# State-space stage of three of four token pairs moved beside the attention steps of a perceiver block

## The reference

```python
# 1. cross attention, for each of 8 batches: context (1024, 256), latents x (64, 256)
ln = _layernorm(latents); kv_input = concat([_layernorm(x), ln])
logits = einsum('bhld,bhsd->bhls', q * scale, k * scale)        # 16 heads of 64
out = softmax(logits) @ v ; return out @ Wo
# 2. state space model over the 64 tokens of a batch, 512 channels, 16 states
xc, z = split(layernorm(x) @ W_in);  xc = silu(conv4(xc));  dbc = xc @ x_proj_w
dt = softplus(dbc[..., :1] * dt_w + dt_b);  A = -exp(A_log)
h = exp(dt * A) * h + dt * B_t * x_t ;  y_t = einsum('bdn,bn->bd', h, C_t)
return ((y + xc * D) * silu(z)) @ W_out + residual
# 3. eight experts (256 -> 1024 -> 256, gelu) on listed tokens, scattered back with weights
```

## Time and profile before

| | us |
|---|---|
| median of 3 runs (lowest, highest) | 875.82 (875.15, 876.38) |
| the profiled execution, its own time | 878.02 |
| its span, first to last instruction | 876.3 |
| attention, 40.5 to 603.7 | 563.2 |
| state space, 603.7 to 789.0 | 185.3 |
| experts and end, 789.0 to 876.3 | 87.3 |

### The profile page before, as it was taken

One profiled execution on the slowest core, in us unless ns is written; L12 is line 12 of the kernel. 1 busy time (PEld: TensorE's weight loads), 2 busy tenths in 40 slices (PEclk: granted clock), 3 DMA queues, 4 the chain that ended last, 5 costly groups with the idle time before them and its releaser, 6 DMA issues.

```text
span 876.3 us, 13897 instructions
## 1 busy us (share of the span) xinstructions
PE 797.1 (91%) x5395; PEld 685.5 (78%) x5395; DVE 501.2 (57%) x1087; ACT 393.7 (45%) x947; POOL 263.2 (30%) x207
## 2 busy tenths in 40 slices
PE   4989999999999999999999999996837788889996
PEld 2679999999999999999999999995313233358895
DVE  5266465565466556456556554444687899970112
ACT  2445454544454554454554354441644444414341
POOL 2818017016105403501801700001045776620000
PEclk8999999999999999999999999998958999999998
DMA  9100100100010010010030010000200000081720
GB/s 312 59 1 1 55 1 1 54 2 2 1 55 2 1 55 1 1 56 1 2 127 1 4 8 2 1 1 3 96 1 0 1 0 0 1 287 31 262 93 27
DMA packets 23781, 35.28 MB, mean 40 GB/s; under 512 B 6744, under 2 KB 19616, under 8 KB 22688
## 3 DMA queue, kind: packets, MB, share of 16 engines
q1 hardware_dynamic: 23712, 34.34, 11.9%
HBM read 32.77 MB, written 0.52 MB: 38 GB/s over the span
## 4 chain that ended last, share of the span: by engine, by line
PE 76%; DVE 11%; issue 7%; POOL 2%; ACT 2%; DMA 1%; SPq 0%; DVEq 0%; POOLq 0%
PE psum L1182 21%; PE psum L1216 19%; PE psum L1199 6%; PE psum L1155 3%; PE psum L1508 3%; PE psum L1498 3%; PE psum L1238 3%; DVE read L805 2%; PE psum L1138 2%; PE psum L1310 2%; PE psum L1377 2%; PE psum L1162 2%; POOL drive L558 2%; PE psum L1248 2%; PE psum L1229 2%
## 5 line engine op out<-in xcount | busy, mean ns | idle before, releaser
L929 ACT ACTIVATE pt_hi<-psum 128x512 fp32r<-128x512 f32 (+1 forms) x192 | 87.3, 489 | 225.7 <-PE psum L1199 170.4
L1216 PE MATMUL psum<-kvn_hi,pt_hi 128*128 128x256 f32 x512 | 149.6, 292 | 0.0
L1216 PE MATMUL psum<-kvn_hi,pt_lo 128*128 128x256 f32 x512 | 144.1, 281 | 0.0
L1216 PE MATMUL psum<-kvn_lo,pt_hi 128*128 128x256 f32 x512 | 143.9, 281 | 0.0
L651 DVE TENSOR_REDUCE rowmax<-psum 128x1 f32<-128x728 f32 x64 | 58.6, 915 | 110.9 <-PE psum L1182 110.9
L558 POOL TENSOR_TENSOR drive<-dtx,b_all 128x512 f32<-128x512 f32 x64 | 82.9, 1301 | 49.0 <-DVE state L796 23.4
L1216 PEld LDWEIGHTS psum<-kvn_lo,pt_hi 128*128 128x128 f32 x512 | 97.2, 190 | 0.1
L1216 PEld LDWEIGHTS psum<-kvn_hi,pt_hi 128*128 128x128 f32 x512 | 97.1, 190 | 0.1
L1216 PEld LDWEIGHTS psum<-kvn_hi,pt_lo 128*128 128x128 f32 x512 | 97.0, 189 | 0.0
L1182 PE MATMUL psum<-kvt_hi,qk_hi 128*128 128x364 f32 (+1 forms) x384 | 90.8, 345 | 4.5 <-ACT prob L969 2.7
L1182 PE MATMUL psum<-kvt_hi,qk_lo 128*128 128x364 f32 (+1 forms) x384 | 85.5, 331 | 0.0
(11 more groups left out here) (205 smaller groups left out, 1494.7 us busy)
## 6 DMA issues: line engine op xcount, KB each, us to landing
w<-in_L_ffn_W_dram SPq DMA_DIRECT2D x16, 1024.0 KB, 7.5
ctx_nat<-in_ctx_dram SPq DMA_DIRECT2D x8, 1024.0 KB, 5.3
wk_nat<-in_L_xattn_Wkv_dram SPq DMA_DIRECT2D x1, 1024.0 KB, 6.1
wq_sb<-in_L_xattn_Wq_dram SPq DMA_DIRECT2D x1, 1024.0 KB, 12.3
wv<-in_L_xattn_Wkv_dram SPq DMA_DIRECT2D x1, 1024.0 KB, 14.4
wo<-in_L_xattn_Wo_dram SPq DMA_DIRECT2D x1, 1024.0 KB, 16.4
lat_cur<-x_lat SPq DMA_DIRECT2D x16, 64.0 KB, 4.9
q_t<-in_L_attn_W_in_dram SPq DMA_DIRECT2D x1, 1024.0 KB, 7.2
```

The source lines that it names most:

```text
L929: act.activation(pt_hi[u][:, t0:t1, :], where[:, 0:(t1 - t0) * P].rearrange("p (t m) -> p t m", m=P), ACT.Copy)\
L1216: pe.matmul(PV, w[u][:, j, :], x_[slot][:, j, :], start=(j == 0 and w is pt_hi and x_ is kvn_hi), stop=False)
```

## The change

The state-space work of pairs 0, 1 and 2 moves into the head steps of later batches; only pair 3 stays behind the attention.

- A unit is now one state of one pair: 4 channel tiles x 128 tokens, again 512 elements a partition. `unit_step` puts one unit in each of the head steps 26 to 57 (pairs 0 and 1), and two in each of the steps 58 to 65 (pair 2). Pair 3 has 16 units after the attention, with a loop like the one before.
- A unit beside the attention is: SP loads its row of B and of C from device memory, repeated over the partitions (`load_rows`, 128 KB); POOL makes the drive (`open_unit`); ACT makes the decay in SBUF with four exponentials (`decays`); DVE scans, with both inputs in SBUF (`scan_unit`); POOL multiplies with C and adds to the sum (`close_unit`, two operations).
- The work around the units of a pair stands at set steps after its base (19, 35, 51): norm and transposes (+1), `in_proj` (+2), convolution (+2, +3), the gate of the convolution (+4), `x_proj` (+5), dt (+5, +6), skip (+7), gate z (+12, +13; +8, +9 for pair 2), gating of the result and product with W_out (+23, +24). Silu is made of an exponential, a plus one, a DVE reciprocal of 128x512 (`invert`) and a product on POOL: two reciprocals a pair.
- Queries (`q_keep`), latents (`latt_keep`, `x_keep`) are stored to device memory and loaded by SP for each batch; this removes POOL's `queries` and ACT's `own_rows` after batch 0. qk has one buffer in place of two, and two of a batch's eight `misc` turns move into that batch's own steps 0 and 1.
- POOL's context work is cut up: norm at hp 2, a quarter of weight and bias at each of hp 3 to 6, high part at 6, low part at 7, latents at hp 0 of the next batch.

```diff
-    UNITS = DT * NS
...
+    TURNS = (0, 2, 4, 5, 6, 7, 1, 3)
+    EARLY, OWN_LATE, NEXT_LATE = {6: 5, 7: 7}, {0: 1, 1: 3}, {3: 0, 4: 2, 5: 4, 6: 6}
...
+    WORKS = 3
+    ROWS = 3
+    INLINE = TT - 1
...
+        def unit_step(u):
+
+            t, n = divmod(u, NS)
+            if t < INLINE - 1:
+                return 2 * HP * t + 26 + n
+            return 2 * HP * t + 26 + n // 2
...
+            def load_rows(u):
+
+                t, n = divmod(u, NS)
+                if u >= ROWS:
+                    sp.wait_ge(v_acc, u - ROWS + 1)
+                pair = dbc_keep[t % 2, 1:, :].rearrange("(a w n) p -> a w n p", a=1, n=NS)[:, :, n, :]
+                sp.dma_start(bc[u % ROWS][:], pair.to_broadcast((P, 2, P))).then_inc(ld_bc[u % ROWS], 16)
...
+            def open_unit(u):
+
+                t, n = divmod(u, NS)
+                pool.wait_ge(ld_bc[u % ROWS], 16 * (u // ROWS + 1))
+                if n == 0:
+                    pool.wait_ge(v_dtx, t + 1)
+                if u >= WORKS:
+                    pool.wait_ge(v_acc, u - WORKS + 1)
+                pool.tensor_tensor(work[u % WORKS][:], dtx[:], bc[u % ROWS][:, 0:1, :].to_broadcast((P, DT, P)),
+                                   ALU.mult).then_inc(v_drv, 1)
+
+            def close_unit(u):
+
+                t, n = divmod(u, NS)
+                pool.wait_ge(v_scan, u + 1)
+                link(pool.tensor_tensor(work[u % WORKS][:], work[u % WORKS][:],
+                                        bc[u % ROWS][:, 1:2, :].to_broadcast((P, DT, P)), ALU.mult))
+                if n == 0:
+                    pool.wait_ge(v_y0, t + 1)
+                else:
+                    pool.wait_ge(v_acc, u)
+                pool.tensor_tensor(y_sum[:], y_sum[:], work[u % WORKS][:], ALU.add).then_inc(v_acc, 1)
...
+                for u in units_at.get(g - 1, ()):
+                    close_unit(u)
+                for u in units_at.get(g, ()):
+                    open_unit(u)
...
+            def invert(t, made, done):
+
+                dve.wait_ge(made, t + 1)
+                dve.reciprocal(gate[:], gate[:]).then_inc(done, 1)
...
+            def scan_unit(u):
+
+                dve.wait_ge(v_dec, u + 1)
+                dve.wait_ge(v_drv, u + 1)
+                flat = "p d m -> p (d m)"
+                dve.tensor_tensor_scan(work[u % WORKS][:].rearrange(flat), dec[u % 2][:].rearrange(flat),
+                                       work[u % WORKS][:].rearrange(flat), 0.0, ALU.mult, ALU.add).then_inc(v_scan, 1)
...
+                for u in units_at.get(g, ())[:1]:
+                    scan_unit(u)
...
+                for d in range(DT):
+                    last = act.activation(seqs(dec[u % 2][:])[:, d, :, 1:], seqs(dts[:])[:, d, :, 1:], ACT.Exp,
+                                          scale=a_neg[:, d, n:n + 1])
+                last.then_inc(v_dec, 1)
...
+            pool.wait_ge(s_woe, TT)
+            token_norm(INLINE)
+            for u in units_at[HP * B + 1]:
+                close_unit(u)
+            times_gate(INLINE - 1)
+            link(pool.memset(zero[:], 0.0))
```

More of the change, by code:

```diff
@@ L206, in perceiver_kernel @@
[L206 to L218 removed]
+        zero = sb(mam, "zero", [P, 2, DT * BP])
@@ L219, in perceiver_kernel @@
+        state = [sb(open_, f"state{i}", [P, DT, P]) for i in range(STATES)]
+        read = [sb(open_, f"read{i}", [P, DT, P]) for i in range(2)]
+        y_skip = sb(open_, "y_skip", [P, DT, P])
+        open_.close()
         xg_t = sb(mam, "xg_t", [P, CK, E, P])
         hid = sb(mam, "hid", [P, FT, P])
-        sb(mam, "rest_of_res", [P, FT, P])
-        oper = ExitStack()
-        dts = sb(oper, "dts", [P, DT, T])
-        dtx = sb(oper, "dtx", [P, DT, T])
-        xc = sb(oper, "xc", [P, DT, T])
@@ L227, in perceiver_kernel @@
-        zs = sb(oper, "zs", [P, DT, T])
-        state = [sb(oper, f"state{i}", [P, T]) for i in range(STATES)]
-        read = [sb(oper, f"read{i}", [P, T]) for i in range(2)]
-        oper.close()
         coef_slot = sb(mam, "coef_slot", [P, E])
@@ L673, in step @@
-                if more and hp == MISC - 1:
-                    misc_lo(b + 1, 1 - slot, hp)
+                    dve.tensor_tensor(x1[:, pair, :], x1[:, pair, :], MB[:, 0:C], ALU.add).then_inc(s_woe, 1)
+                t = pair_at(g, 1)
+                if t is not None:
+                    token_turn(t)
+                t = pair_at(g, 4)
+                if t is not None:
+                    invert(t, v_e1, v_rcp)
+                t = gate_pair(g, 13)
+                if t is not None:
+                    invert(t, v_ez1, v_rz)
@@ new lines, in step @@
+                if t is not None:
+                    token_stats(t)
+                if more and hp < 2:
+                    ctx_stats(b + 1, hp)
+                job = late_turn(b, hp, more)
+                if job:
+                    misc_lo(job[0], job[0] % 2, job[1])
+                if more and hp == 2:
+                    ctx_scale(b + 1)
+                for u in units_at.get(g, ())[1:]:
+                    scan_unit(u)
+                t = pair_at(g, 1)
+                if t is not None:
+                    turned_in(t)
@@ L1250, in out_proj, with turn_tokens, in_proj @@
                     last.then_inc(s_wo, 1)
+            def turn_tokens(t, now):
+                pe.wait_ge(v_xn, t + 1)
+                pe.wait_ge(s_lB, count(now[0], now[2]))
+                xn_ = gate[:].rearrange("p d m -> p (d m)")
+                for k in range(CK):
+                    last = pe.transpose(TP[1][:, k * P:(k + 1) * P], xn_[:, k * P:(k + 1) * P], ident[:])
+                last.then_inc(v_xt, 1)
+            def in_proj(side, where):
+                for d in range(DT):
+                    for k in range(CK):
+                        col = (side * DT + d) * P
+                        last = pe.matmul(where[:, d * P:(d + 1) * P], win[:, k, col:col + P], xn_t[:, k, :],
+                                         start=(k == 0), stop=(k == CK - 1))
+                return last
@@ L1276, in step @@
                     head_out(p3)
-                if more and hp < MISC - 1:
-                    misc(b + 1, 1 - slot, hp, pair + 1 if slot == 0 and hp == 3 and pair is not None else None)
+                free_bank(b, hp)
+                job = late_turn(b, hp, more)
+                if job:
+                    misc(job[0], job[0] % 2, job[1], pair + 1 if slot == 0 and hp == 3 and pair is not None else None)
             def body(b, slot, more, pair):
```

1076 lines of the change are left out of this document (663 added, 413 removed).

## The result

The changed kernel takes **866.4 us** (median of 4 runs, 863.1 to 868.6) against 876.1 us for the kernel before in the same session: a ratio of 0.9883, 95% interval 0.9847 to 0.9920. The forecast was 811 us, range 782 to 846. So the change is faster, as forecast, and by more than the interval, but by 1.2% where I had said 7%; with a limit of 2% it would count as no change.

What follows compares the result with a forecast made beforehand. PE was taken to bound the attention, with room on every other engine. Attention ending at 649 us, units and rest 74, experts 87.3 gave a span of 810.3; forecast 811 us, range 782 to 846.

Steps and rivals of the forecast that it cites:

- The tail: Behind the attention: one pair's preparation, loop of 16 units and the rest, 32.3 + 31.2 + 10.5 = 74.0 us for 185.3.
- (d): POOL in steps 58 to 65: 5.15 us a unit, 10.3 us a step with two; attention's end 24.3 us later.
- the shared door: DVE operations with both inputs in SBUF and POOL's operations exclude each other; 19.5 us of (d) for 16 scans.
- rival 1: Cheap cover: scan and POOL share nothing in practice, reciprocal a plain pass; G 14 us, time 780 us; chance 0.17.
- (b): DVE's scan in steps with one unit: 1.22 us, fitting in DVE's idle room, so costed at nothing.
- (c): Six DVE reciprocals of 512 elements beside the attention: 1 us each, 6 us in all.
- (e): POOL in batches 4 and 6: 71 us of work for 70 us of batch; 3 us in each, 6 us.
- My own sign: Over 75 us between batch starts before step 58 would show that (e) is dearer than forecast.
- (a): PE's new products for the pairs: 9 us ahead of step 58, counted in full.
- Rival 2: Dear cover: reciprocals over 4 us, POOL 8 us late in both crowded batches; G 73 us, time 845; chance 0.25.
- G: Growth of the attention stage by the work moved beside it: 9 + 6 + 24.3 + 6 = 45 us.
- Rival 3: Clock: PE's gaps lower its granted clock, 5.4 us a head step over (d); 12 such steps cancel the gain; chance 0.05.

Runs made afterwards that it cites:

- run 6: Changed kernel with the 48 scans beside the attention run over one column in place of 512 (recurrence left out): 840.1 us, 0.9589.
- run 7: Changed kernel with scan and POOL's three operations of each of the 48 inline units on one column in place of 512: 817.2 us, 0.9322.
- run 8: Changed kernel with the first product of pair 2's 16 units made on DVE just ahead of the scan, in place of POOL: 860.3 us, 0.9802.
- Run 5: Changed kernel with two more waits on POOL, so its context work waits for the convolution taps; no work taken out: 859.4 us, 0.9798.
- run 2: Changed kernel with the first batch's high and low parts waiting for their own group's count again: 859.6 us, 0.9805.

## Why the prediction was wrong

**Right.** The tail: POOL's tables ahead of xn_t, both tables of 4.4 us, the taps (4.24 us for 4.3) and the loop (30.6 us for 31.2). One term was missed there, most of the 4.5 us by which the first scan is late, the last line of this POOL timeline:

```profile
734.81 1.26 POOL L757 TENSOR_TENSOR drive<-dtx_l,b_all 128x512 f32<-128x512 f32 x1 [3.75 <-DMA b_all<-dbc_keep]
```

The rows of B go through device memory, which I had "cost at nothing": the first scan is 36.8 us behind the attention for 32.3. Behind the loop it is 12.0 for 10.5. Beside the attention POOL waited for a row pair nine times, 14.6 us in all (5.35 us in step 57, 3.07 in step 41); how much of that reached the end is not shown.

**Right: step (d), the shared door.** "A step with two takes 10.3 us": the mean of steps 58 to 62 is 11.0, and from step 58 to the end it is 27.0 us for 24.3. Of the 27.0, 11.2 lie behind the row maximum of step 63, where the granted clock was 0.82, and (d) had no term for the clock; that the total came out so near is in part luck. Runs 6, 7 and 8 bear it out against rival 1: scans alone are worth 28.6 us, and where a scan meets POOL's operation it takes 2.2 us for 1.2. What I had not counted is that PE itself needs 8.6 us a step there (gate z's products), and the late row pairs. The Trainium skill ("SBUF — State Buffer", who interferes with whom) calls the pair of ports an exclusive lock, and says of the two-port modes that it is held for the whole instruction; the taps with two SBUF inputs behave so here, 4.74 us for 0.87.

**Wrong: steps (b), (c) and (e), the cover of the single steps.** I had the shared door, and then used it only where POOL was full. In the single steps I weighed busy time against room ("I take nothing", "1 us each", "3 us in each"), by batch, 71 of 70 us (the terms as written add up to 69.6). My own sign for it came: from batch start to batch start over 75 us, and batches 4 and 6 took 88.4 each, 71.4 before. Lateness does not come from a batch's sum. It comes from which of DVE's operations meets which of POOL's within a step: taps against the context, the scan of step 38 against its high part, the reciprocal (3.33 us, not 1) in the same step as a blocked scan. Batches 2 to 6 grew by 55.7 us; 15.3 us were PE's products (five of the six halves of `in_proj` and what goes with them), and for the other 40, 31.5 of gaps and 8.9 of the lower clock, I had the 12 of (c) and (e). Run 5 took 6 us out by order alone. The Trainium skill ("VectorE: DVE Perf Modes", the fixed hardware budget) had led me to an estimate of 4.3 us for the reciprocal, which I left as the upper end; the measured 3.33 lies nearer to it than to the 1 us I took from the pass of 0.66.

**Wrong: step (a).** I read "x8" in the earlier trace rows as eight products. A product of this kind is two records: `in_proj` has 16 a pair and shows 32. PE's new work is 20.3 us, not 12, and I counted 9 of it ahead of step 58, where 15.3 had come by step 56.

**Missed: the start.** The table of turns stood in the diff, and its use in the first batch's waits changed what they wait for. That is 6.8 us by the medians of run 2, and 8.0 of the 9.1 us by which step 16 was late, in a place that I had costed at nothing.

**The rivals.** Rival 1 is refuted (runs 6 and 7). Rival 2's range (830 to 873) holds the time, but its G of 73 us does not; its costly reciprocals came true at 3.33 us instead of over 4, and the engine that PE waited for in the crowded batches was DVE, held up by POOL, and not POOL itself. Rival 3's mechanism is there in part: four steps (38, 39, 54, 55) ran partly at the lower level, each with a gap of PE of 3 to 5 us, and so did the start and the stretch behind step 63, 19.0 us of PE's busy time in all. Its 5.4 us a step for 12 steps were not reached; in the steps with two units the clock stayed at 1.00, though PE was busy for only 46.5 of 55.1 us. What I had set against it, that only gaps of several us stand beside low clocks, misread the trace of before: in its unit loop the clock is 0.50 over 727.8 to 731.2, behind a gap of 1.74 us that ends at 725.66. I had left this out of the forecast's own range, as if the clock fell everywhere or nowhere.

**Open.** The split into 31.5 us of gaps and 8.9 of the clock is read from the profile; it was not tried apart by a run. Some of the gaps may themselves follow from the slower products ahead of them. To try it would take products that fill PE's gaps without touching a bank that another engine is using. Whether scan and taps would be free of POOL with one input in PSUM, as the scan of before was, could not be tried either: no bank stands free for it beside the attention.

## What to carry to other kernels

When work is moved beside other work, lay the steps out one by one and ask which operation meets which; a room of 30% as an average says nothing where two engines take turns, and the first late step then costs a gap and the clock behind it. Keep operations with both inputs in SBUF on VectorE apart in time from GpSimd's, by a wait on GpSimd if need be. Shortening the scans gave 28.6 us here and shortening the taps nothing: the wait for the other engine's operation stays. And where a table of numbers changes, follow every wait that is counted by it, those that run once too: a gap whose length does not move with the load can be one of them.
